# The first FFN stream of a three-stage block: normalisation and value bias on other engines, half-tile sums, a new order

## The reference

```python
x = x + 0.5 * ffn(ln(x), Wr, We)        # first stage, with the projections of the attention
x = x + attention(ln(x), Wq, bq, Wk, bk, Wv, bv, Wo, bo)   # 16 heads of 16, rotary
x = x + 0.5 * ffn(ln(x), Wr, We)        # third stage

def ffn(x, Wr, We):                     # 8 experts, each 256 x 256
    logits = x @ Wr.T
    top_vals, top_idx = top_k(logits, 2)
    w = softmax(top_vals)
    # a token's place among those that chose the same expert; beyond the capacity it is dropped
    keep = place < int(4096 * 2 / 8 * 1.5) + 1
    return sum_k(w_k * keep_k * (x @ We[top_idx_k]))
```

## Time and profile before

| | |
|---|---|
| median of 3 runs | 6545.29 us (6541.36 to 6547.69) |
| the profiled execution's own time | 6538.67 us |
| its span, first to last instruction | 6536.8 us |
| TensorE busy in the span | 6260.8 us (96%) |
| VectorE busy | 6022.9 us (92%) |
| ScalarE busy | 4749.2 us (73%) |
| GpSimd busy | 378.0 us (6%) |
| first stage, to the last instruction of its work on VectorE | 769.9 us |

### The profile page before, as it was taken

How to read it: one execution, slowest core, us unless ns; L and a number is a source line. 1 busy time by engine, 2 the same in 40 slices (tenths; PEclk the granted TensorE clock), 3 DMA queues, 4 the chain that set the end, 5 groups by cost and what they waited for, 6 DMA issues and landing times. The chain is left out here.

```text
span 6536.8 us, 158115 instructions
## 1 busy us (share of the span) xinstructions
PE 6260.8 (96%) x54288; PEld 2794.2 (43%) x54288; DVE 6022.9 (92%) x6989; ACT 4749.2 (73%) x8697; POOL 378.0 (6%) x604
## 2 busy tenths in 40 slices
PE   7888599999999999999999999999999999998998
PEld 5666433333333333333333333333333333334776
DVE  7888599999999999999999999999999999992776
ACT  2222138888888888888888888888888888885111
POOL 2322300000000000000000000000000000001221
PEclk9999779999999999999999999999999999999999
DMA  2222401010000101010101010101010101000110
GB/s 81 88 91 93 100 11 16 13 17 17 13 16 13 20 10 20 10 20 10 20 10 20 10 22 12 20 10 23 13 16 13 16 13 16 4 20 29 51 46 27
DMA packets 120628, 174.85 MB, mean 27 GB/s; under 512 B 61760, under 2 KB 78672, under 8 KB 116944
## 3 DMA queue, kind: packets, MB, share of 16 engines
q1 hardware_dynamic: 120144, 167.19, 11.2%
HBM read 97.93 MB, written 69.21 MB: 26 GB/s over the span
## 5 line engine op out<-in xcount | busy, mean ns | idle before, releaser
L1020 DVE TENSOR_REDUCE at_mx<-at_m 128x1 f32<-128x1024 f32 x4070 | 4975.9, 1223 | 82.0 <-PE at_m L954 38.3
L995 ACT ACTIVATE at_ex<-at_s 128x512 f32<-128x512 f32 x8192 | 4449.0, 595 | 715.7 <-PE at_s L905 144.6
L905 PE MATMUL at_s<-at_q,at_k 50*128 50x512 f32 x8192 | 2995.5, 444 | 0.0
L884 PE MATMUL at_m<-at_k,at_q 48*128 48x512 f32 x8032 | 2923.9, 443 | 1.0 <-DVE at_mx L1020 1.0
L915 PE MATMUL at_po<-at_ex,at_v 128*32 128x256 f32 x32816 | 2623.6, 391 | 31.7 <-POOL at_v L853 31.7
L884 PEld LDWEIGHTS at_m<-at_k,at_q 48*128 48x128 f32 x8032 | 1183.1, 185 | 1657.1 <-DVE at_mx L1020 1596.8
L915 PEld LDWEIGHTS at_po<-at_ex,at_v 128*32 128x32 f32 x32816 | 646.3, 108 | 1519.0 <-issue 746.4
L905 PEld LDWEIGHTS at_s<-at_q,at_k 50*128 50x128 f32 x8192 | 1211.2, 185 | 42.7 <-ACT at_ex L995 42.3
L299 PE MATMUL fr_ps<-sh_weh,fr_xl 128*128 128x512 f32 x512 | 179.7, 433 | 115.9 <-DVE fr_acc L470 115.9
L859 POOL COPY at_v<-at_vst 128x1024 f32<-128x1024 f32 x16 | 16.7, 1041 | 4557.7 <-DMA at_vst<-v_by_head 4557.7
L1279 PE MATMUL bk_ps<-sh_weh,bk_xl 128*128 128x512 f32 x512 | 169.0, 411 | 23.5 <-DVE bk_acc L1404 23.5
(11 more groups left out here) (169 smaller groups left out, 2802.8 us busy)
## 6 DMA issues: line engine op xcount, KB each, us to landing
at_q<-q_parts SPq DMA_DIRECT2D x96, 256.0 KB, 4.9
at_k<-k_parts SPq DMA_DIRECT2D x96, 256.0 KB, 6.3
q_parts<-fr_parts SPq DMA_DIRECT2D x64, 256.0 KB, 2.2
k_parts<-fr_parts SPq DMA_DIRECT2D x64, 256.0 KB, 2.4
attended<-at_o SPq DMA_DIRECT2D x256, 34.0 KB
fr_x<-in_x SPq DMA_DIRECT2D x16, 512.0 KB, 4.2
after_ffn<-fr_acc SPq DMA_DIRECT2D x16, 512.0 KB, 3.0
v_by_head<-fr_v SPq DMA_DIRECT2D x16, 512.0 KB, 4.1
```

Source lines behind the costliest of these rows:

```text
L884: ins = pe.matmul(pm[w][:, h * QB:(h + 1) * QB], Q[p][rows, base + i * P:base + (i + 1) * P], K[p][rows, c * CW + h * QB:c * CW + (h + 1) ...
L905: pe.matmul(ps[event(t) % NS], K[p][rows, j * P:(j + 1) * P], Q[p][rows, sb_ * QU + g * QB:sb_ * QU + (g + 1) * QB], start=True, stop=True ...
L995: ac.activation(Ex[QUAD * (j % NX) + 2 * g + 1 - half][:, :], ps[event(t) % NS], ACT.Exp)\
L1020: ve.tensor_reduce(out=mx[u][:, i, c:c + 1], in_=first[(v * RED + k) % len(first)][:, 0:CW] if opening else pm[w][:, :], op=ALU.max, axis= ...
```

## The change

Normalisation (`normal`) is parted. `newton` on VectorE makes the small instructions, now six: the sixth gives `nb = -mean * rs`. `normalise` on ScalarE makes the four 128x256 instructions as `rs * x + nb`. The value bias enters by TensorE: `values` begins each tile with a product of a two-row `one_r` and a two-row `bvp`, whose rows hold the high and the low part of the bias; `take_values` on ScalarE copies v out. The two rows are made once, in the prologue. `lower` on GpSimd subtracts in four pieces of 128x256. `combine` takes a range of experts, and other work stands between its halves. Chunk 15 goes into bank 1; with that, chunk 0 of the next group waits only for chunk 12's sums. `room` moves to the end of the body, ahead of the next statistics, and `positions` moves ahead of the second rotary product on TensorE.

The diff, cut to what is spoken of:

```diff
@@ -119,8 +119,11 @@
+    BANK = [n % NB for n in range(CHUNKS - 1)] + [1]
+    PIECE = GT // 2
+    NEWTON = 6
...
@@ -290,13 +296,14 @@
-                        if n == 0:
-                            need(pe, s_ac, g * STEPS)
+                        if n < 2:
+                            need(pe, s_ac, g * STEPS - (0 if n else EP * NB))
-                            pe.wait_ge(s_ac, g * STEPS + EP * (n - NB + 1))
+                            last_use = max(m for m in range(n) if BANK[m] == BANK[n])
+                            pe.wait_ge(s_ac, g * STEPS + EP * (last_use + 1))
-                                last = pe.matmul(pe_s[n % NB][:, :], (xh, xl)[a][0][u][:, c, i * P:(i + 1) * P],
+                                last = pe.matmul(pe_s[BANK[n]][:, :], (xh, xl)[a][0][u][:, c, i * P:(i + 1) * P],
@@ -318,11 +325,12 @@
+                        half = pq[i // 2][:, (i % 2) * D:(i % 2 + 1) * D]
+                        pe.matmul(half, one_r[:, :], bvp[:, :], start=True, stop=False)
-                                last = pe.matmul(pq[i // 2][:, (i % 2) * D:(i % 2 + 1) * D],
-                                                 (xh, xl)[a][1][0][:, c, i * P:(i + 1) * P], (wvh, wvl)[b][:, c, :],
-                                                 start=(t == 0 and c == 0), stop=(t == len(SPLIT) - 1 and c == NC - 1))
+                                last = pe.matmul(half, (xh, xl)[a][1][0][:, c, i * P:(i + 1) * P], (wvh, wvl)[b][:, c, :],
+                                                 start=False, stop=(t == len(SPLIT) - 1 and c == NC - 1))
@@ -330,6 +338,8 @@
+                pe.wait_ge(s_bv, 5)
@@ -350,10 +360,10 @@
                         router(g + 1)
                     if runs(g, 0):
                         experts(g, u, 3)
+                    if runs(g, 1):
+                        positions(g + 1)
                     if runs(g, -1):
                         rotary(g - 1, 1)
-                    if runs(g, 1):
-                        positions(g + 1)
                 iterations(pe, body)
@@ -362,6 +372,23 @@
+                def normalise(k, n, src):
+                    need(ac, s_nw[k], (n + 1) * NEWTON)
+                    need(ac, s_tr[k], n)
+                    for i in range(TG):
+                        last = ac.activation(xn[k][:, i, :], src[:, i, :], ACT.Identity, bias=nb[k][:, i:i + 1],
+                                             scale=rs[k][:, i:i + 1])
+                    last.then_inc(s_xn[k], 1)
+                def take_values(n):
+                    need(ac, s_v, n + 1)
+                    need(ac, s_sv, n * DMA)
+                    for i in range(TG):
+                        last = ac.activation(vt[:, :, i, :], pq[i // 2][:, (i % 2) * D:(i % 2 + 1) * D]
+                                             .rearrange("p (h d) -> p h d", d=HD), ACT.Copy)
+                    last.then_inc(s_vc, 1)
...
@@ -410,8 +438,12 @@
                         evacuate(g - 2, 1)
                     if runs(g, -1):
                         take_root(1, g - 1)
+                        normalise(1, g - 1, acc[1 - u])
+                    if runs(g, -2):
+                        take_values(g - 2)
                     if runs(g, 1):
                         take_root(0, g + 1)
+                        normalise(0, g + 1, xg[1 - u])
                     if runs(g, -1):
                         turned(1, g - 1, 0)
                     if runs(g, -2):
@@ -439,27 +471,26 @@
-                def normal(k, n, src):
+                def newton(k, n):
-                    ch = Chain(ve, s_nw[k], 5, n)
+                    need(ve, s_xn[k], n)
+                    ch = Chain(ve, s_nw[k], NEWTON, n)
+                    ch.add(ve.scalar_tensor_tensor(out=nb[k][:, :], in0=mv[k][:, :, 0], scalar=-1.0, in1=rs[k][:, :],
+                                                   op0=ALU.mult, op1=ALU.mult))
-                    need(ve, s_tr[k], n)
-                    for i in range(TG):
-                        last = ve.tensor_scalar(xn[k][:, i, :], src[:, i, :], mv[k][:, i, 0:1], rs[k][:, i:i + 1],
-                                                ALU.subtract, ALU.mult)
-                    last.then_inc(s_xn[k], 1)
-                def combine(g, u, it, i):
-                    if i == 0:
+                def combine(g, u, it, i, first, end):
+                    if i == 0 and first == 0:
-                    for e in range(E):
+                        need(ve, s_xn[1], g - 1)
+                    for e in range(first, end):
...
@@ -550,8 +573,20 @@
+                ve.wait_ge(s_k, 4 * DMA)
+                ve.wait_ge(s_bv, 1)
+                ve.tensor_copy(one_r[:, :], ones2[:, 0:P]).then_inc(s_bv, 1)
+                bias = Chain(ve, s_bv, None, None)
+                bias.n = 2
+                bias.settle()
+                bias.step(ve.tensor_copy(bvp[:, :], bv2[:, :]))
+                ve.tensor_tensor(bvl[:, :], bv2[:, :], bvp[:, :].bitcast(F32), ALU.subtract)
+                bias.step(ve.tensor_scalar(bvt[:, :], bvp[:, :].bitcast(F32), ident[0:2, 0:1], None, ALU.mult))
+                bias.step(ve.scalar_tensor_tensor(out=bvp[:, :], in0=bvl[:, :], scalar=ident[0:2, 1:2], in1=bvt[:, :],
+                                                  op0=ALU.mult, op1=ALU.add))
+                room(0)
@@ -560,25 +595,26 @@
                     if runs(g, -2):
                         low(g - 2, 0)
                     if runs(g, 0):
-                        room(g)
-                        combine(g, u, it, 0)
+                        combine(g, u, it, 0, 0, E // 2)
+                    if runs(g, -1):
+                        newton(1, g - 1)
+                    if runs(g, 0):
+                        combine(g, u, it, 0, E // 2, E)
                     if runs(g, -2):
                         products(g - 2, u, it - 1, 1)
-                    if runs(g, -1):
-                        normal(1, g - 1, acc[1 - u])
-                    if runs(g, -2):
-                        add_bias(g - 2)
                     if runs(g, 1):
                         hold(ve, s_x[1 - u], (it + u) * DMA + DMA, s_tick)
                         statistics(0, g + 1, xg[1 - u])
                     if runs(g, 0):
-                        combine(g, u, it, 1)
+                        combine(g, u, it, 1, 0, E // 2)
+                    if runs(g, 1):
+                        newton(0, g + 1)
+                    if runs(g, 0):
+                        combine(g, u, it, 1, E // 2, E)
                     if runs(g, -2):
                         rotate(g - 2, 1)
-                    if runs(g, 1):
-                        normal(0, g + 1, xg[1 - u])
                     if runs(g, 0):
-                        combine(g, u, it, 2)
+                        combine(g, u, it, 2, 0, E)
                     if runs(g, -2):
                         low(g - 2, 1)
                     if runs(g, -1):
@@ -586,11 +622,15 @@
                     if runs(g, 1):
                         pick(g + 1)
                     if runs(g, 0):
-                        combine(g, u, it, 3)
+                        combine(g, u, it, 3, 0, E // 2)
+                    if runs(g, 1):
+                        odds(g + 1)
+                    if runs(g, 0):
+                        combine(g, u, it, 3, E // 2, E)
                     if runs(g, -1):
                         rotate(g - 1, 0)
                     if runs(g, 1):
-                        odds(g + 1)
+                        room(g + 1)
                 iterations(ve, body)
@@ -598,8 +638,12 @@
-                    gp.tensor_tensor(xl[k][u][:, :, :], xt[k][:, :, :], xh[k][u][:, :, :].bitcast(F32), ALU.subtract)\
-                      .then_inc(s_xl[k], 1)
+                    for c in range(NC):
+                        for h in range(GT // PIECE):
+                            cols = slice(h * PIECE, (h + 1) * PIECE)
+                            last = gp.tensor_tensor(xl[k][u][:, c, cols], xt[k][:, c, cols],
+                                                    xh[k][u][:, c, cols].bitcast(F32), ALU.subtract)
+                    last.then_inc(s_xl[k], 1)
```

More of the change, by code:

```diff
@@ L138, in front_phase @@
         wvh, wvl = sb("wvh", [P, NC, D], F32R), sb("wvl", [P, NC, D], F32R)
-        bqk, bv, bs = sb("bqk", [P, 4]), sb("bv", [P, D]), sb("bs", [P, 4])
+        bqk, bs = sb("bqk", [P, 4]), sb("bs", [P, 4])
+        bv2, bvh, bvl, bvt, ones2 = (sb(n, [2, D]) for n in ("bv2", "bvh", "bvl", "bvt", "ones2"))
+        bvp, one_r = sb("bvp", [2, D], F32R), sb("oner", [2, P], F32R)
         xg = [sb(f"x{u}", [P, TG, D]) for u in range(2)]
@@ L147, in front_phase @@
         mv = [sb(f"mv{k}", [P, TG, 2]) for k in range(2)]
-        var, root, r0, r1, rs = ([sb(f"{n}{k}", [P, TG]) for k in range(2)] for n in ("var", "root", "r0", "r1", "rs"))
+        var, root, r0, r1, rs, nb = ([sb(f"{n}{k}", [P, TG]) for k in range(2)]
+                                     for n in ("var", "root", "r0", "r1", "rs", "nb"))
```

(18 more changed lines are left out.)

## The result

The changed kernel takes 6492.38 us (median of 4 runs, 6490.44 to 6502.21); the kernel before, measured beside it, 6543.32. The ratio of the means is 0.9928, 95% interval 0.9911 to 0.9945: 51 us less in the medians, 47.1 in the spans of the profiled executions (6536.8 to 6489.7). The forecast was 84 less, 6461 us, with a range from 6434 to 6487. The direction was right; the time lies 5 us outside the range.

A forecast was written before the change was run, and what follows sets the result against it. VectorE was taken to set the 45.83 us group; at 39.9, thirteen periods save 77 us, groups 1 to 2 4, group 0 1, the drain 3, less 1.4 for the prologue: 84 off 6545.29, so 6461 us, range 6434 to 6487.

The forecast's parts named there:

- The loop: First stage, each group: VectorE's products, choice and four sums, then TensorE's unbroken list; 38.5 us, 39.9 with the clock.
- One wait replaces four: TensorE, ahead of chunk 15: one bank wait of 3.6 us per group replaces four of up to 2.97.
- the odd half: VectorE's wait for the odd rotary half, 2.59 us before, was to stay at 2 to 3 us.
- stall of fr_rs: VectorE's four-element operation, 2.33 us beside GpSimd's subtraction: 2.2 us go per group, by the order of the work.
- The bias product: TensorE, in values: four two-row matmuls of 256 columns cost 0.46 us a group, between nothing and 0.8.
- The clock: TensorE restarts at half clock after seven in ten of the new waits, costing 1.4 us per group.
- Rival (a): The clock falls in every group, for 3.1 us: 41.6 us a group, 6483 us in all; chance 20%.
- Rival (c): GpSimd's pieces at the shared port lengthen the loop by 2.2 us: 42.1 a group, 6490 us; chance 7%.
- The drain: After the last group, rotation no longer waits for VectorE's bias addition behind the last values: 3 us saved.
- The small terms: Outside the 13 periods: groups 1 to 2 save 4 us, group 0 saves 1, the prologue's bias chain costs 1.4.
- ScalarE is late: ScalarE's normalisation comes late for the transposes and the change does nothing, within 0.2% of before; chance 3%.
- The slower case: The one long wait takes the clock for most of the group: at 30 us, 53.5 a group, 6638 us; chance 3%.

The follow-up runs named there:

- e6: Changed kernel with GpSimd's subtraction as one instruction again instead of four pieces; 6489.53 us, ratio 0.9924 to the kernel before.
- e3: Changed kernel plus ten unread products on TensorE between chunks 14 and 15, filling its wait; 6488.01 us, ratio 0.9923.
- e2: Changed kernel with the bias product at 128 rows (126 of bvp zero) instead of two; 6464.41 us, ratio 0.9883.
- e5: Changed kernel with chunk 15 back in bank 0, waiting for chunk 12's sums; 6470.95 us, ratio 0.9896.
- e11: Changed kernel with the second rotary product ahead of chunk 15, and statistics and low parts behind tile 0's first half; 6452.05 us, ratio 0.9860.
- e1: Changed kernel without the two-row bias products, so v lacks its bias; 6464.96 us, ratio 0.9886.
- e12: Changed kernel's order with the 128-row bias product and chunk 15 in bank 0; 6442.71 us, ratio 0.9846.
- e7: Changed kernel with the eight normalising instructions back on VectorE, bias and order kept; 6505.78 us, ratio 0.9947.
- e10: The kernel of e11 with the 128-row bias product of e2; 6465.79 us, ratio 0.9879.
- e8: Changed kernel plus eight unread products on TensorE between chunks 14 and 15; 6474.65 us, ratio 0.9895.

## Why the prediction was right in direction and too large

**The loop: right.** "One wait replaces four", of 3.6 us ahead of chunk 15: 3.46. VectorE still waits for the odd half, 2.87. No weights wait, no stall of fr_rs, and the stall went by the order and not by the pieces (e6). ScalarE at 2.08 and 1.21 us, both under cover. With the clock at 1.00 and the bias at its true cost the loop is 40.16 (e3), where the prediction's own terms with 2.0 for the bias give 40.04.

**The bias product: the step that failed.** The price was taken as 0.46 a group with 0.8 as its upper bound; it is 2.0. The bound was wrong as a bound: it went by the nearest rows in columns, and none of these rows had another number of rows than its neighbours. 13 x 1.54 = 20 us of the 84 are lost here, and some 4 more in the drain (e2 against e3, e5 and e6, below).

**The clock: mechanism right, size off.** Forecast were seven restarts in ten, 1.4 us a group. Each of the 13 periods is 1.4 to 2.3 above the 40.16 of e3, on average 1.9: 13 x 0.5 = 7 us. The Trainium skill, TensorE: Matmul & The Clock Gate, section "A second HAM failure mode: psum-queue depth-cycling", named in the prediction, has the clock swing where TensorE idles shortly between groups of matmuls. The trace agrees for one wait of 3.5 us in a turn, with a fall in each turn, but not for e11, where up to three waits of 0.2 to 1.3 us stand in each group and the clock stays at 1.00. Rival (a), 41.6 us and 6483, took the fall in every group but 3.1 us for it, and has the bias at 0.46. Rival (c), 42.1 us and 6490, comes nearest to the measured 42.07 and 6492.38, and that is chance: its 2.2 us at the port are not there (products and choice 5.86, and e6), and bias and clock happen to add up to as much.

**The drain: wrong sign.** Three us were to be saved there; 12.7 - 2.7 = 10 are lost. The two sets of values last 7.95 and some 8.4 us in place of 2.84 and 4.6. But the first set is long mainly by the clock, and not in each kernel with two-row products. TensorE's timeline of e6, which keeps them:

```profile
689.02 0.38 PE L329 MATMUL fr_pq<-fr_bvp,fr_oner 2*128 2x256 f32 x1 [1.77 <-ACT fr_odd L407]
...
695.07 1.09 PE L272 MATMUL fr_pT<-sh_ident,fr_xn 128*128 128x128 f32 x8 [1.14 <-ACT fr_xn L381]
```

Here the set is over after 4.9 us, at full clock throughout, and so it is in e3 and e5. From the last mark to the attention these three take 81.4 to 82.0 in place of 86.7; with 128 rows (e2) it is 77.7. So some 4 us of the drain are the product's, and some 5 are the clock of the first set and a stall: in the last group VectorE stood still for 2.38 us ahead of its first sum without a releaser in the profile (e1 2.37, e3 1.54, e2 1.28; in e5, e6 and e12 a wait of 1.3 to 1.9 for a chunk of TensorE stands there). What it waited for stays open, and so do the 1.6 us by which e2 is still behind the kernel before (77.7 against 73.4 + 2.7).

The small terms nearly held: by the marks groups 1 to 2 saved 4.1 (forecast 4) and groups 0 to 1 3.5 (1), by the first sums 3.2 and 1.9; the start lost 2.4 (1.4). The 5.7 us that the rest of the kernel gave were not forecast. Together: -84 + 20 (bias) + 8 (clock, and a loop 0.1 longer) + 13 (drain, 10 + 3) + 2.7 (mark) - 2.5 (groups 0 to 1, where the mark's 2.7 come back) + 1 (start) - 5.7 (the rest of the kernel) = -47.5, against the 47.1 by which the spans differ.

**The rivals.** That the change did nothing, that ScalarE is late and that the port takes back 2.2 us are refuted by the rows above. The slower case, a clock lost for most of the group, did not come; the longest stretch of a group with a granted clock below 1.00 is 6.8 us.

## What to carry to other kernels

A matmul's price is read from a row with the same neighbours as much as from one with the same columns: a small product of two rows set between large ones cost four times what the same product with 126 rows of zeros did, and on the engine that had just become the bound. When a change hands the bound to another engine, what it adds there counts in full and what it still removes on the first counts nothing in the loop (e7). And on TensorE a wait is worth a price of its own: less work in front of a wait can make it longer and the kernel slower, as in e10, so it is the length of the waits that is to be planned, not only the sum.

## What the runs showed of the hardware

- A float32r product of 256 columns: 0.12 us with 128 rows among products of 128 rows, 0.50 with two rows in the same place (a group's four: 2.0 against 0.5).
- The clock after a wait of TensorE in this stage: behind 3.46 us it fell in all groups, for 1.9 us on average; behind 2.3 to 2.8 it fell in 11 of 13 groups in e5, for 1.4 a group, and in seven in e12, for 0.4; behind 2.7 to 3.0 in e10 in ten of 13; behind 0.6 to 1.6 (e3, e8, e11) in none. What decides at the same wait stays open. The fall can also come a us or two behind a restart whose first pair still takes 0.73. And the length of the wait isn't all of it: in e3's attention the clock fell for 37 us behind a stall of 1.11.
- In the drain a set of values with two-row products lasts 4.9 us at full clock (e6) and 7.95 mostly at the lower level (after). e2's sets, with 128 rows, fall and regain the clock after some 3.4 us; e11's first, with two rows, does the same (649.2 to 652.7), while both of the changed kernel stay low to their end. Whether the rows have a part in that is not shown.
- The attention, 5.2 ms of unchanged code, took between 5228.5 and 5255.4 us over these kernels (5228.5 to 5237.9 without e3), the last stage 527.0 to 531.2. A gain of under ten us in one stage is therefore to be read in that stage, not in the total.
